# Context channels as 128 plus a doubled rest of 64, and both ends of a transformer-block kernel reordered

## The reference

```python
attn_in = adaln(x, cond, ln1, g1, b1)                # layer norm, then scale and shift from cond
x = attn(attn_in, attn_in, sa_wq, sa_wkv, sa_wo, sa_bo) + x
cross_in = adaln(x, cond, ln1, g1, b1)
ctx_n = ln(context, ca_lnc_w, ca_lnc_b)              # 192 channels
x = attn(cross_in, ctx_n, ca_wq, ca_wkv, ca_wo, ca_bo) + x
ffn_in = adaln(x, cond, ln2, g2, b2)
x = gelu(ffn_in @ ff_w1 + ff_b1) @ ff_w2 + ff_b2 + x
```

## Time and profile before

| | |
|---|---|
| median of 3 runs | 1118.23 us |
| the profiled execution | 1118.14 us |
| its span in the trace | 1116.3 us |
| TensorE busy | 1095.8 us (98%) |
| VectorE busy | 852.1 us (76%) |
| GpSimd busy | 779.4 us (70%) |
| ScalarE busy | 636.8 us (57%) |
| mean granted TensorE clock | 0.993 of full |

### The profile page before, as it was taken

The page is one execution under the profiler, slowest core; times in us unless marked ns, Lnnn a source line. Parts: engine busy times, 40 slices in busy tenths (PEclk is TensorE's granted clock), DMA queues, the critical chain, the costliest instruction groups (busy, mean ns, idle before and its releaser), DMA issues.

```text
span 1116.3 us, 18288 instructions
## 1 busy us (share of the span) xinstructions
PE 1095.8 (98%) x6904; PEld 784.4 (70%) x6904; DVE 852.1 (76%) x1019; ACT 636.8 (57%) x895; POOL 779.4 (70%) x503
## 2 busy tenths in 40 slices
PE   8799999999999999999999999999999999989998
PEld 7567666677666776666776667776666776756997
DVE  5787887877787777888888777777877777777444
ACT  5475565665566555577665555555555545776521
POOL 3498887787778767789799766767777667765210
PEclk9899999999999999999999999999999999999999
DMA  5222121311231111211121112211131111300001
GB/s 169 80 51 68 28 53 39 90 30 30 53 77 38 39 38 21 72 39 39 29 63 38 39 39 55 56 24 35 38 72 39 38 30 30 114 1 1 20 19 38
DMA packets 59542, 52.31 MB, mean 47 GB/s; under 512 B 22976, under 2 KB 42432, under 8 KB 59200
## 3 DMA queue, kind: packets, MB, share of 16 engines
q1 hardware_dynamic: 57568, 49.57, 18.5%
q10 hardware_dynamic: 1888, 1.59, 0.5%
HBM read 15.22 MB, written 2.10 MB: 16 GB/s over the span
## 4 chain that ended last, share of the span: by engine, by line
PE 91%; DVE 3%; ACT 2%; DMA 2%; issue 1%; SPq 0%; POOL 0%; ACTq 0%; DVEq 0%; POOLq 0%
PE ps L855 18%; PE ps L701 12%; PE ps L702 11%; PE ps L703 11%; PE ps L800 6%; PE ps L843 6%; PE ps L833 5%; PE ps L806 5%; PE ps L802 5%; PE ps L804 5%; PE ps L946 4%; PE ps L717 1%; DMA x<-x_dram 1%; DVE lo L1055 0%; DVE tmp L1064 0%
## 5 line engine op out<-in xcount | busy, mean ns | idle before, releaser
L539 ACT ACTIVATE probs<-ps 128x1024 f32<-128x1024 f32 x256 | 262.5, 1027 | 203.2 <-PE ps L806 178.8
L1037 DVE TENSOR_REDUCE neg_max<-ps 128x2 f32<-128x1024 f32 x256 | 301.6, 1225 | 78.4 <-PE ps L833 78.4
L414 POOL TENSOR_TENSOR acc<-acc,probs 128x1024 f32<-128x1024 f32 x128 | 307.0, 2398 | 18.7 <-POOL acc L409 0.4
L855 PE MATMUL ps<-probs,v 128*64 128x512 f32 x1024 | 230.7, 592 | 0.0
L409 POOL TENSOR_TENSOR acc<-probs 128x1024 f32<-128x1024 f32 x64 | 153.1, 2392 | 74.8 <-ACT probs L539 74.8
L855 PEld LDWEIGHTS ps<-probs,v 128*64 128x64 f32 x1024 | 73.6, 137 | 145.7 <-issue 145.7
L419 POOL TENSOR_TENSOR eo<-tmp 128x512 f32<-128x512 f32 x62 | 87.6, 1413 | 111.8 <-DVE tmp L1064 111.5
L1064 DVE TENSOR_TENSOR tmp<-ps,rope 128x1024 f32<-128x1024 f32 x128 | 150.5, 1211 | 3.9 <-PE ps L703 3.2
L800 PE MATMUL ps<-max_rows,pick 64*128 64x512 f32 x512 | 109.6, 420 | 4.3 <-DVE o_lo L1051 2.7
L833 PE MATMUL ps<-hi 64*128 64x512 f32 x512 | 105.1, 401 | 5.2 <-ACT hi L553 2.9
L701 PE MATMUL ps<-xn_hi,w_hi 128*128 128x512 f32 x256 | 107.3, 419 | 2.1 <-DVE xn_lo L289 1.1
(11 more groups left out here) (117 smaller groups left out, 2248.9 us busy)
## 6 DMA issues: line engine op xcount, KB each, us to landing
...
x<-x_dram SPq DMA_DIRECT2D x4, 512.0 KB, 7.4
...
max_rows<-neg_max SPq DMA_DIRECT2D x128, 2.0 KB, 2.0
...
out<-x SPq DMA_DIRECT2D x4, 512.0 KB, 2.9
...
```

The lines of the kernel that those rows point to most:

```text
L414: pool.tensor_tensor(acc[:, g % 2, :, :], acc[:, g % 2, :, :], probs[:, i, :, :], ALU.add).then_inc(added, 1)
L539: act.activation(probs[:, i, :, :], score_ps(i), ACT.Exp, scale=SCALE).then_inc(exped, 1)
L855: mm = pe.matmul(av_ps[DH * h:DH * h + DH, :], v[:, u % 2, kt, c:c + DH], probs[:, kt, h, :], start=(kt == 0), stop=(kt == TT - 1))
L1037: dve.tensor_reduce(neg_max[:, g % 2, :, i], peak_ps(i), AX.X, ALU.max, negate=True).then_inc(maxed, 1)
```

## The change

**Context tiles.** The context becomes one tile of 128 channels and one of the remaining 64, and these 64 stand twice, on partitions 0 to 63 and 64 to 127; weights and layer-norm vectors are loaded the same way (`LOADS` goes from 7 to 11 DMAs for a phase-1 weight load), and ScalarE writes the last 64 channels of each scaled context row a second time. A phase-1 key job is now `project` with 6 matmuls, and `project_rest` with 6 more that run as three pairs on the two array halves, e = 0 on one, e = 1 on the other. The values likewise: 12 matmuls in `project_v`, 12 in `project_v_rest` as six pairs. Both rests stand at the end of the period, behind `project_out`, and only they signal `projected` and `v_projected`.

**The head.** GpSimd, not VectorE, turns job 0; job 1 is rotated into its own buffer; job 2 is projected into banks 0 and 2, ahead of `modulate(2)`; the norm of sequence 2 comes ahead of `project(3)`; the low parts of sequence 1's norm go from GpSimd to VectorE, and `add_bias(0)` moves into period 0; the two DMAs of `land` have a semaphore each, and `high_qk(0)` stands ahead of `guess_rstd(2)`.

**The end.** In period 61 VectorE runs `low_o(60)` ahead of the layer norm's statistics; the splitting of the MLP weights (`split_ffw`) moves to other places in periods 60 to 62; `total(60)` goes to bank 4 and waits for a reduce. The last `mlp` finishes its last three blocks for tokens 0 to 255 first, then for the others, and `add_y` and the store go by halves.

```diff
+        def tmp_of(j):
+            return probs[:, 2:4, :, :] if j == 1 else tmp
...
-            return ps[:, 6 if g == PAIRS - 1 else 0, :]
+            return ps[:, {PAIRS - 1: 6, PAIRS - 4: 4}.get(g, 0), :]
...
-            return ps[:, 3 + e, :]
+            return ps[:, (0, 2)[e] if j == 2 else 3 + e, :]
...
-                        for kt in range(KT):
-                            at = KT * 128 + kt * 256
-                            sp.dma_start(raw[0:CK, 1:3, kt, a, :],
-                                         pack[0:CK, at:at + 256].rearrange("p (m c) -> p m c", m=2))\
+
+                        first, second = KT * 128, KT * 128 + 256
+                        for rows, kt, src, at in ((slice(0, CK), 0, slice(0, CK), first),
+                                                  (slice(CK, 128), 0, slice(0, 128 - CK), second),
+                                                  (slice(0, 64), 1, slice(128 - CK, CK), second),
+                                                  (slice(64, 128), 1, slice(128 - CK, CK), second)):
+                            sp.dma_start(raw[rows, 1:3, kt, a, :],
...
-                    sp.dma_start(raw_qk[:, g % 4, k, :], eo_of(j)[64 * a:64 * a + 64, :, :]).then_inc(landed, 16)
+                    sp.dma_start(raw_qk[:, g % 4, k, :], eo_of(j)[64 * a:64 * a + 64, :, :]).then_inc(landed[a], 16)
...
-                sp.wait_ge(y_added, b + 1)
-                sp.dma_start(out_d[b].rearrange("(t p) d -> p t d", p=128), x[:, b, :, :]).then_inc(stored, 16)
-            sp.wait_ge(stored, 16 * NB)
+                for r in range(2):
+                    sp.wait_ge(y_added, 2 * b + r + 1)
+                    sp.dma_start(out_d[b, 256 * r:256 * r + 256].rearrange("(t p) d -> p t d", p=128),
+                                 x[:, b, 2 * r:2 * r + 2, :]).then_inc(stored, 16)
+            sp.wait_ge(stored, 32 * NB)
...
-            pool.wait_ge(rows_in, 16)
-            add_bias(0)
-            norm_split(pool, 1, 0)
-            norm_split(pool, 1, 1)
+            rotate(0)
+            pool.wait_ge(ln_split, 4)
+            low_weights(pool, 0, 3)
             refine_rstd(pool, 2)
...
+                    if order[n][0] == C:
+                        act.activation(z[:, tt, DC:D], src[:, tt, 128:DC], ACT.Identity, bias=centre[:, tt:tt + 1],
+                                       scale=rstd[:, tt:tt + 1])
+                    act.activation(z[:, tt, 0:src.shape[-1]], src[:, tt, :], ACT.Identity, bias=centre[:, tt:tt + 1],
...
-                act.wait_ge(landed, 32 * (2 * (g // 2) + 2))
+                act.wait_ge(landed[g % 2], 16 * (2 * (g // 2) + 2))
...
+                if p == PAIRS - 2:
+                    for c in range(4):
+                        split_ffw(1, c)
...
-                if k == 1 and phase == 1:
-                    rows, a_hi, a_lo = CK, ctx_hi, ctx_lo
-                else:
-                    rows, a_hi, a_lo = 128, xn_hi, xn_lo
+                whole = k == 0 or phase == 0
+                a_hi, a_lo = (xn_hi, xn_lo) if whole else (ctx_hi, ctx_lo)
                 for e in range(2):
-                    if 0 < j < 4:
+                    if j in (1, 3):
                         pe.wait_ge(roped, 2 * (j - 1) + e + 1)
                     if j == 3 and e == 1:
                         pe.wait_ge(maxed, 3)
-                    for kt in range(KT):
+                    for kt in range(KT if whole else 1):
                         c = slice(kt * 256 + e * 128, kt * 256 + (e + 1) * 128)
-                        mm = parts(job_ps(j, e), w_hi[0:rows, k, c], w_lo[0:rows, k, c],
-                                   a_hi[0:rows, b, kt, :], a_lo[0:rows, b, kt, :], kt == 0, kt == KT - 1)
-                    mm.then_inc(projected, 1)
+                        mm = parts(job_ps(j, e), w_hi[:, k, c], w_lo[:, k, c], a_hi[:, b, kt, :], a_lo[:, b, kt, :],
+                                   kt == 0, whole and kt == KT - 1)
+                    if whole:
+                        mm.then_inc(projected, 1)
+
+
+
+            halves = (slice(0, 64), slice(64, 128))
+
+            def project_rest(j):
+                u = j // 2
+                b = quad(u)[1]
+                for n, (w_, a_) in enumerate(((w_hi, ctx_hi), (w_hi, ctx_lo), (w_lo, ctx_hi))):
+                    for e, half in enumerate(halves):
+                        c = slice(256 + e * 128, 256 + (e + 1) * 128)
+                        mm = pe.matmul(job_ps(j, e), w_[half, 1, c], a_[half, b, 1, :], start=False, stop=(n == 2))
+                        if n == 2:
+                            mm.then_inc(projected, 1)
...
-                rows, a_hi, a_lo = (CK, ctx_hi, ctx_lo) if phase == 1 else (128, xn_hi, xn_lo)
+                a_hi, a_lo = (ctx_hi, ctx_lo) if phase == 1 else (xn_hi, xn_lo)
                 for t in range(2):
                     cut = slice((2 * r + t) * 128, (2 * r + t + 1) * 128)
-                    for kt in range(KT):
-                        c = slice(kt * 256, (kt + 1) * 256)
-                        mm = parts(v_ps(u, r)[:, t * D:(t + 1) * D], a_hi[0:rows, b, kt, cut], a_lo[0:rows, b, kt, cut],
-                                   w_hi[0:rows, 2, c], w_lo[0:rows, 2, c], kt == 0, kt == KT - 1)
-                mm.then_inc(v_projected, 1)
+                    out = v_ps(u, r)[:, t * D:(t + 1) * D]
+                    if phase == 0:
+                        for kt in range(KT):
+                            c = slice(kt * 256, (kt + 1) * 256)
+                            mm = parts(out, a_hi[:, b, kt, cut], a_lo[:, b, kt, cut], w_hi[:, 2, c], w_lo[:, 2, c],
+                                       kt == 0, kt == KT - 1)
+                    else:
+                        for n, (a_, w_) in enumerate(((a_hi, w_hi), (a_hi, w_lo), (a_lo, w_hi))):
+                            pe.matmul(out, a_[:, b, 0, cut], w_[:, 2, 0:256], start=(t == 0 and n == 0), stop=False,
+                                      skip_group_check=True)
+                if phase == 0:
+                    mm.then_inc(v_projected, 1)
+
+            def project_v_rest(u):
+                b = quad(u)[1]
+                for t in range(2):
+                    for n, (a_, w_) in enumerate(((ctx_hi, w_hi), (ctx_hi, w_lo), (ctx_lo, w_hi))):
+                        for r, half in enumerate(halves):
+                            cut = slice((2 * r + t) * 128, (2 * r + t + 1) * 128)
+                            mm = pe.matmul(v_ps(u, r)[:, t * D:(t + 1) * D], a_[half, b, 1, cut], w_[half, 2, 256:512],
+                                           start=False, stop=(n == 2), skip_group_check=True)
+                            if t == 1 and n == 2:
+                                mm.then_inc(v_projected, 1)
...
+                if g == PAIRS - 4:
+                    pe.wait_ge(maxed, 4 * (g + 2) + 3)
+                elif is_pair(g + 1):
...
+                if is_job(p + 4) and p % 2 == 0 and quad((p + 4) // 2)[2] == 1:
+                    project_rest(p + 4)
+                if p in v_in and quad(v_in[p])[2] == 1:
+                    project_v_rest(v_in[p])
...
+            project(2)
             modulate(2)
-            project(2)
             peak(0, 0)
             peak(0, 1)
+            modulate(3)
             peak(0, 2)
             peak(0, 3)
-            modulate(3)
-            project(3)
             norm(2, 0)
             norm(2, 1)
+            project(3)
...
+                    blocks(0, FT - 3)
+                    for tokens in (range(2), range(2, TT)):
+                        for f in range(FT - 3, FT):
+                            down(f, tokens)
...
-                if p in stats_in:
+                if p in stats_in and p != PAIRS - 3:
                     norm_stats(stats_in[p])
+                    norm_means(stats_in[p])
                 if is_pair(p - 1):
                     low_o(p - 1)
+                if p == PAIRS - 3:
+                    norm_stats(stats_in[p])
+                    norm_means(stats_in[p])
+                if p == PAIRS - 2:
+                    for c in range(4):
+                        split_ffw(0, c)
...
-            turn(0)
             rotate(1, 0)
             rotate(1, 1)
             turn(1)
+            norm_split(dve, 1, 0)
+            norm_split(dve, 1, 1)
             norm_stats(2)
             rotate(2, 0)
             rotate(2, 1)
+            norm_means(2)
...
-                dve.wait_ge(y_step, 8 * b + 8)
-                rows = x[:, b, :, :].rearrange("p t d -> p (t d)")
-                dve.tensor_tensor(rows, ps[:, 4:6, :].rearrange("p a n -> p (a n)"), rows, ALU.add)\
-                   .then_inc(y_added, 1)
+                for r in range(2):
+                    if b < NB - 1:
+                        dve.wait_ge(y_step, 8 * b + 8)
+                    else:
+                        dve.wait_ge(y_half, r + 1)
+                    rows = x[:, b, 2 * r:2 * r + 2, :]
```

(2 more changed lines are left out.)

87 lines of the change are left out of this document (57 added, 30 removed).

## The result

The changed kernel takes 1159.61 us (median of 4 runs, 1157.83 to 1161.53), the kernel before 1118.16: a ratio of 1.0371, 95% interval 1.0358 to 1.0384. The forecast was slower, by 22 us; it is 41. The profiled execution took 1157.83 us with a span of 1156.0, against 1118.14 and 1116.3 before, so the comparison of the two traces explains 39.7 us.

What follows compares the result with a forecast made beforehand. TensorE, busy 1095.8 of 1116.3 us, was taken as the bound. 1118.1 + 26.7 - 10.6 + 14.4 + 0.5 - 6.5 - 1.1 - 1.1 = 1140.4 us, range 1120 to 1154.

Steps and rivals of the forecast that it cites:

- key jobs and value projections: Sixteen each in phase 1: key jobs cost 1.67 us each, +26.7 us; value projections save 0.66 each, -10.6 us.
- clock: Behind the sixteen holds: granted clock falls to 1.2 GHz nine times, 1.6 us each, +14.4 us (0 to +25.6).
- queues (context norms): Extra weight-load DMAs on SyncE taken at 0; ScalarE's extra context-row pieces in four periods +0.5 us (0 to +5).
- head: Before the first scores: the 2.91 us idle time goes and part of the slow clock returns, -6.5 us (-8.7 to -2).
- period 61 and end: Earlier low_o(60) in period 61, -1.1 us; halved last add and store, -1.1 us.
- The hold: TensorE idle at the odd periods' first peak, waiting for VectorE's rotations and first add_out: 2.33 us, sixteen times.
- ScalarE's two copies fit under the 0.93 us of the first score: Value jobs: v is complete later, but ScalarE's copies of it lie under the first score.
- Value pairs: Value rest: six half-array pairs of 256 columns at 0.13 us each, saving 0.66 us per value job.
- The 8 us: Value pairs: if two 128-column weight loads take 213 ns a pair, the saving is 0.16 us, the sum 8 us higher.
- the rival in which it stays: Phase 1: TensorE is held but the clock does not fall, 1126.0 us (1119 to 1131); chance 0.22.
- Every hold brings a fall: Phase 1: all sixteen holds drop the clock, 1.6 us each, 1151.6 us; chance 0.18.
- v is complete later in the period: Value projections: the value tile is whole later, but ScalarE's two copies fit under the first score's 0.93 us.

Runs made afterwards that it cites:

- Experiment 2: The changed kernel with the key rest moved directly behind the key tile, ahead of the output projection: 1107.04 us, ratio 0.9899 to the kernel before.
- experiment 5: The kernel before, without context tiles, with only the context key job moved behind the output projection: 1161.65 us, ratio 1.0388.
- experiment 8: Experiment 7's kernel with TensorE's first peak one step later in the sixteen even periods behind a context value job: 1109.77 us, ratio 0.9923 to the kernel before.
- experiment 3: The changed kernel with nine extra unread products filling the hold ahead of the first peak, in twelve of sixteen odd periods: 1149.98 us, ratio 1.028.
- experiment 7: Experiment 2's kernel with value rest directly behind value tile, context norms' z behind o_hi and av, lo of pair 1 behind second modulation: 1099.77 us.
- 4: The changed kernel with VectorE adding the output projection ahead of rotating the key job, in periods with a context key job: 1135.99 us, ratio 1.0148.
- 6: Experiment 2's kernel with the value rest's six products of rows 0 to 63 issued before those of rows 64 to 127: 1108.40 us, ratio 0.9903.
- experiment 1: Two halves of the change, each on the kernel before: only the context tiles, 1160.07 us, ratio 1.0368; only the reordered head and end, 1115.75 us, ratio 0.998.

## Why the prediction was wrong

The direction and the mechanism were right, the size was not: the terms of the sum miss 17.4 us between them. By its own terms, against the profiled executions:

| term | predicted | measured |
|---|---|---|
| key jobs and value projections | +26.7 - 10.6 = +16.1 | +24.7 |
| clock | +14.4 (9 falls of 1.6) | +14.0 (9 of 1.55) |
| queues (context norms) | +0.5 | +3.0 |
| head | -6.5 | -2.4 |
| period 61 and end | -1.1 - 1.1 | +0.4 |
| sum | +22.3 | +39.7 |

The 24.7 is what 38.7 leaves without 14.0. This term has the largest miss, 8.6 us; the head has 4.1, the context norms 2.5, period 61 and the end 2.6. The median lies another 1.8 us above the profiled execution. No trace shows where, but the granted clock is 0.979 in the profiled execution and 0.975 to 0.978 in the slower ones, which points at further falls of 1.55 us each.

**The hold** was where and nearly what was said: 2.38 against 2.33 us, at the peak's first pair, by L1165, sixteen times. Experiment 2 shows that the place behind the output projection makes it, and experiment 5 that it is shorter where the two halves of the job end one after the other.

**Key and value jobs, mis-sized by about half a microsecond a pair of periods.** In the steady part it costs 1.50 us a pair where the prediction has 1.67 - 0.66 = 1.01. Three pieces of it can be read. Behind the hold the peak pair is followed only after 0.43 us (790.60 to 791.03) instead of 0.23. The same happens at the other first peak, in the even period, which meets its wait for v without a visible idle time; TensorE in the changed kernel:

```profile
771.77 0.39 PE L815 MATMUL ps<-w_hi,ctx_hi 64*128 64x256 f32 x2
771.99 0.28 PE L815 MATMUL ps<-w_lo,ctx_hi 64*128 64x256 f32 x2
772.11 0.28 PE L815 MATMUL ps<-w_hi,ctx_lo 64*128 64x256 f32 x2
...
772.58 0.40 PE L865 MATMUL ps<-max_rows,pick 64*128 64x512 f32 x2
772.82 0.39 PE L867 MATMUL ps<-hi 64*128 64x512 f32 x2
...
773.51 0.61 PE L900 MATMUL ps<-hi 64*128 64x512 f32 x2
773.94 0.43 PE L865 MATMUL ps<-max_rows,pick 64*128 64x512 f32 x2
```

And the output projection's first product, right behind the end of `low_o` (782.81 + 0.69 = 783.50), is followed after 0.23 (783.55 to 783.78) instead of 0.12. That is 0.20 + 0.20 + 0.11 = 0.5 us a pair, less the 0.1 that the first score behind a value job gains (772.58 to 772.82, against 0.35 in the earlier trace rows), since the switch now lies ahead of the rest; the sum counted that for the key jobs alone. About 0.1 us of the 0.5 is left unread. So the first step that failed is the price of a wait's end: the sum let TensorE go on at 0.23 or 0.12 us behind every wait, and it loses 0.1 to 0.2 us more at each of three a pair. The second is "ScalarE's two copies fit under the 0.93 us of the first score", which put the even period's first peak among them: the pairs end both halves of v together, so both copies start at the period's end. Before, ScalarE's first copy ran ahead of it, while the second half was projected:

```profile
718.34 0.59 ACT L571 COPY v<-ps 128x512 f32<-128x512 f32 x1 [3.30 <-PE ps L703]
719.77 0.59 ACT L571 COPY v<-ps 128x512 f32<-128x512 f32 x1 [0.85 <-PE ps L703]
```

and in the changed kernel (the period that ends at 772.58) the two stand in one row:

```profile
772.78 1.07 ACT L599 COPY v<-ps 128x512 f32<-128x512 f32 x2 [4.19 <-PE ps L815]
```

The peak at 773.51 needs the first of them, which ends at about 773.37. In experiment 8, where that peak comes 0.93 us later and v is long there, the pair is a normal one; but no time was to be had in that way.

**Value pairs** were right: the pairs above stand 0.11 to 0.12 us apart, a value job takes 772.58 - 770.24 = 2.34 instead of 2.98 us, 0.64 saved of 0.66 predicted. The Trainium skill gives the time of one weight load, columns / 1.2 ns (TensorE: Matmul & The Clock Gate, "LDWEIGHTS (loading the stationary operand)"), which is 107 ns for 128 columns. That two loads into the two row halves add up to 0.213 us was the prediction's step, and the trace refutes it: a pace of 0.12 us has room for one such load and not for two, one behind the other. The 8 us did not come.

**The clock** was right in kind and in the price of a fall, and the rival in which it stays is refuted. The idle time brings the falls (experiment 3). That nine were counted and nine came is luck: the nine had no working behind it, and the kernel with the tiles alone had ten. "Every hold brings a fall" is refuted as well, though the time is even above its 1151.6: ten times at most, out of sixteen, in the kept traces.

**The queues.** The term for the context norms took the four extra pieces at 0 to 5 us and chose 0.5. They stand in ScalarE's queue ahead of o_hi, for which o_lo and then `project_out` wait, and they cost 3.0; moved behind it they cost nothing (experiment 7). The bound was right and the choice was not: VectorE's 0.65 us of waiting for it in the earlier trace rows says how little slack it has. The DMAs of a weight load were taken at 0, and that was nearly so: they delay the first score of period 35 by 0.50 us, and the hold of that period is shorter by more (1.43 instead of 2.21). Without the holds the same wait is 1.57 us (experiment 2).

**The head.** The old wait of 2.91 us went, and period 0 starts 4.3 us sooner, at 42.37 ("near 41.5"). The clock did not hold: it stands at 0.50 from 34.0 on for 6.8 us instead of 10.2, so that of the 5.1 us only 1.7 came back. As the prediction feared, TensorE has little to do there and waits for the norm of sequence 2:

```profile
36.59 1.97 PE L750 MATMUL ps<-ident,z 128*128 128x128 f32 x8 [1.21 <-ACT z L524]
```

The step that failed is that the gain stays. VectorE in the changed kernel:

```profile
44.47 4.71 DVE L1121 TENSOR_REDUCE neg_max<-ps 128x2 f32<-128x1024 f32 x4 [0.77 <-PE ps L900]
49.10 3.37 DVE L1139 TENSOR_TENSOR lo<-lo,hi 128x1024 fp32r<-128x1024 f32 x1
52.39 1.40 DVE L1106 BATCH_NORM_STATS2 stats<-x 128x6 f32<-128x256 f32 x4
...
54.66 2.34 DVE L1148 TENSOR_TENSOR tmp<-ps,rope 128x1024 f32<-128x1024 f32 x2
```

`low_qk(1)` takes 3.37 us beside GpSimd's adds (L432, from 49.02 for 5.70 us; 1.32 in the steady period at 783.41), the statistics and job 4's rotation stand behind it, and the first peak of period 1 is held for 1.52 us. Here a fall of 3.4 us follows from 57.9 on, but it is not what takes the gain back. Experiments 2, 4 and 6 have the same head and the same hold without a fall, and they too give back 1.9 to 2.0 us up to period 2. Where the fall is absent, TensorE waits for VectorE's reduces instead, as in experiment 2's kernel:

```profile
60.92 0.62 PE L900 MATMUL ps<-hi 64*128 64x512 f32 x2 [1.68 <-DVE neg_max L1121]
```

So VectorE sets the pace of period 1. The prediction followed the head to its first score and not into the two periods behind it.

**Period 61 and the end.** Period 62 gained 0.6 us, but in period 61 the first scores wait 1.12 us for the exponentials, which queue behind the copies of a v that is whole only at the end of period 60 and behind four roundings of weights. That belongs to "v is complete later in the period", which the text judged for the steady periods alone. The reordering by itself was worth what the prediction took: 1.4 us between periods 60 and 63 with the old tiles (experiment 1, ends), and 1.6 with the value rest moved ahead (experiment 7), where the wait of 1.12 us is gone and the four roundings still stand in their place. The halved last add and store (0.69 and 2.3 us against 1.23 and 2.9) show in their rows, but the end as a whole did not shorten: `project_out` of the last job now waits 1.3 us for o_lo. This wait comes with the reordered ends: the kernel with only the ends has it (1.27 us), the one with only the tiles does not. Which of the moves at the end makes it no run tells.
